# Scan stage of a Mamba layer: rows of C broadcast by DMA beside those of B, states written into PSUM

## The chip, the cores and the metric

One core of a Trainium2 chip runs the whole kernel in one launch. The metric is the time of one execution on the device in microseconds (us), measured several times, of which the median counts. The engines are TensorE (PE, its weight loads PEld), VectorE (DVE), ScalarE (ACT) and GpSimd (POOL); SyncE (SP) issues most DMAs.

## The reference, cut to what matters

The kernel computes a patch tokenizer (convolutions and depthwise convolutions on 32 images), a Mamba layer, and an attention layer with a mixture of experts. The change lies in the Mamba layer's selective scan, and touches the end of the tokenizer and the start of attention. There x is 32 sequences of 82 tokens and 192 channels, the inner width is 384, the state has 16 entries:

```python
xdbl = jnp.einsum('bld,kd->blk', z, W_xproj)
dt_in, Bm, Cm = jnp.split(xdbl, [DT_RANK, DT_RANK + D_STATE], axis=-1)
dt = jax.nn.softplus(jnp.einsum('blr,dr->bld', dt_in, W_dt) + b_dt)
A_bar = jnp.exp(dt[..., None] * A)
Bx = (dt * z)[..., None] * Bm[:, :, None, :]
# h[t] = A_bar[t] * h[t-1] + Bx[t], along the sequence
y = jnp.einsum('blds,bls->bld', h, Cm) + D_skip * z
```

## The kernel before

`mamba` works in 8 rounds of 4 sequences (N = 4 x 82 = 328 tokens). The 384 inner channels lie on 128 partitions three times over, so a full row of work is 3 x 328 = 984 elements. A round has 16 steps, one for each entry s of the state:

- ScalarE writes the decays exp(dt A_s) into PSUM banks 0 and 1 (`decays`, L1198), two steps ahead.
- GpSimd computes Bx, dt z times row s of B (`inputs`, L1450), up to three steps ahead in a ring of four tiles. It reads B from the tile `Bb`, in which row s stands on all 128 partitions.
- VectorE runs the scan in two halves of 492 elements (L1333), decays from PSUM and Bx from SBUF, into one of four SBUF tiles `hs`; then it multiplies that tile in place by row s of C (L1343), which it reads from PSUM.
- TensorE adds the product into banks 4 and 5 with an identity matrix (`add_y`, L1050) and, before that, spreads row s+2 of C over 128 partitions into bank 2 or 3, with a bf16 matmul of a one-hot matrix `sel` (`spread_c`, L1030). So that C keeps its precision it comes as three bf16 parts, stacked in the tile `P3` (the profile calls it P): the high part is copied by ScalarE (L1145), the rest R is computed by VectorE (L1289), its copies by ScalarE (L1149, L1150) and the last part by GpSimd (L1416).

Beside the scan of round i, the same 16 steps carry the parts of the round before and after it: `post` of round i-1 (drain of y by ScalarE at step 0, L1216; output projection at step 1, L997, and its addition on VectorE, L1309; norm; gated feed-forward at steps 10 to 13, L955, L1188, L1314, L1317; down projection at step 14, L1022, and additions, L1323) and `pre` of round i+1 (norm; gate and input projections at steps 3 to 5 with z on VectorE, L1285; the projection X at step 6, L979, from which B, C and the input of dt come; softplus in steps 8 to 11 with u by ScalarE, L1157, and four operations of GpSimd). For round 0, `pre` runs at the end of the tokenizer (the `tail` functions and the lines behind `tok.vector`), with softplus on VectorE (L1292 to L1302).

The order of the work on each engine is written out by hand. `program` (one for each engine) calls, for each step, `step`, `post` and `pre` in that order on VectorE and GpSimd, and `post`, `pre`, `step` on TensorE and ScalarE. Engines wait for one another by counting semaphores; a wait holds everything behind it on its engine. Side results use banks 6 and 7 in turn (`SIDE_TILES`, `free`). SP's own program (L887 and on) does, for each round: wait for the rows of B (`Bs`), store them to DRAM (L903), load them back in four groups of four rows, each broadcast to 128 partitions (L907), into one of two halves of `Bb`; then a fill of the experts' buckets with zeros (L917). Behind the last round stand the weight loads for attention (`fr.loads`).

After the last scan, GpSimd's `ending` fills tiles for attention with constants (`fills`, L681 to L685; L683 is the tile kB) and then computes roots for norms (L704).

`Own` and `at_least` are helpers for waits: `at_least` leaves out a wait for a value of zero or less.

## Time and profile before

| | us |
|---|---|
| median of 3 executions | 1364.94 (1364.93 to 1366.9) |
| the profiled execution, its own time | 1364.19 |
| its span, from the first to the last instruction | 1362.2 |
| TensorE busy | 1196.6 (88%) |
| VectorE busy | 1066.6 (78%) |
| ScalarE busy | 710.4 (52%) |
| GpSimd busy | 744.2 (55%) |

Busy times are of the whole span; stages have other shares. The eight rounds of the scan lie between about 253 and 763 us of the span, a round of the middle lasts 64.72 us. Times in the rows below count from the start of the span. In a timeline row stand start, duration, engine, line and operation, output and inputs with partitions x elements, how many instructions are merged (x), and in brackets for how long the engine stood idle before it and whose result ended that.

### The profile page before, as it was taken

The numbers are of one execution on the slowest core, as the hardware profiler recorded it, in microseconds if no ns is written. First come the engines' busy times: TensorE is split into PE (matmuls) and PEld (weight loads), VectorE is DVE, ScalarE is ACT, GpSimd is POOL, SyncE is SP. The second block draws the span as 40 slices with busy tenths as digits, with TensorE's granted clock in tenths as the row PEclk, the third lists the DMA queues.
The fourth block names the chain that finished last, engine by engine and source line by source line (L and its number), as shares of the span: only waits on it lengthen the run. The fifth ranks groups of instructions, "written<-read, shape, count | busy, mean of one in ns | idle before, by whom it ended". The sixth has DMA issues, their size and how long they took to land.

```text
span 1362.2 us, 20654 instructions
## 1 busy us (share of the span) xinstructions
PE 1196.6 (88%) x5844; PEld 759.2 (56%) x5845; DVE 1066.6 (78%) x2275; ACT 710.4 (52%) x1652; POOL 744.2 (55%) x473
## 2 busy tenths in 40 slices
PE   7986867478898989899997789999999889999996
PEld 4432434224454545455452468888888666667674
DVE  5998697998999999999989645677788756666663
ACT  1256431776868777787866334555553462323232
POOL 3047651877878796969697420115545665232322
PEclk9897878698999999999999998999998899999998
DMA  6200002440404041322320025001112133222221
GB/s 186 60 1 0 28 9 63 157 149 1 149 1 149 12 137 39 110 75 74 108 73 1 1 93 186 9 9 25 27 26 56 37 61 54 41 37 39 39 39 21
DMA packets 72573, 81.11 MB, mean 60 GB/s; under 512 B 13450, under 2 KB 65129, under 8 KB 72489
## 3 DMA queue, kind: packets, MB, share of 16 engines
q1 hardware_dynamic: 53154, 69.17, 16.0%
q0 software_dynamic: 17152, 9.24, 5.0%
q10 hardware_dynamic: 2184, 1.72, 0.5%
q8 instruction: 36, 0.59, 0.2%
q14 instruction: 47, 0.39, 0.1%
HBM read 48.75 MB, written 30.01 MB: 58 GB/s over the span
## 4 chain that ended last, share of the span: by engine, by line
PE 56%; DVE 20%; ACT 12%; issue 7%; POOL 2%; DMA 2%; DVEq 1%; SPq 0%; ACTq 0%; POOLq 0%
PE ps L1050 7%; PE ps L2295 6%; DVE hs L1333 5%; PE ps L2273 5%; PE ps L1652 3%; PE ps L1710 3%; PE ps L1022 3%; ACT ps L1198 3%; PE ps L2278 3%; PE ps L277 3%; PE ps L955 2%; PE ps L1725 2%; PE ps L2285 2%; PE ps L270 2%; PE ps L997 2%
## 5 line engine op out<-in xcount | busy, mean ns | idle before, releaser
L1450 POOL TENSOR_TENSOR Bx<-dtz,Bb 128x984 f32<-128x984 f32 x128 | 287.7, 2272 | 47.6 <-DVE hs L1333 34.4
L1333 DVE TENSOR_TENSOR_SCAN hs<-ps,Bx 128x492 f32<-128x492 f32 x256 | 287.7, 1165 | 15.9 <-POOL Bx L1450 12.2
L1050 PE MATMUL ps<-hs,b_id 128*128 128x492 f32 x512 | 236.9, 586 | 8.5 <-ACT y L1216 7.2
L1198 ACT ACTIVATE ps<-dt,A 128x324 f32<-128x324 f32 (+1 forms) x512 | 210.5, 456 | 56.3 <-DVE hs L1333 53.6
L2431 POOL DMA_INDIRECT out<-yt,dest x48 | 74.7, 1556 | 158.9 <-DVE yt L2417 149.2
L2350 ACT ACTIVATE hT__6147<-ps,e_b 128x128 f32<-128x128 f32 x288 | 79.4, 374 | 154.1 <-PE ps L2285 154.0
L1343 DVE TENSOR_TENSOR hs<-hs,ps 128x984 f32<-128x984 f32 x128 | 150.4, 1175 | 2.8 <-issue 0.6
L1050 PEld LDWEIGHTS ps<-hs,b_id 128*128 128x128 f32 x512 | 93.4, 195 | 75.3 <-issue 69.6
L2295 PE MATMUL ps<-W,hT__6147 128*128 x576 | 109.4, 327 | 1.0 <-DVE yb L2411 1.0
L2126 POOL DMA_INDIRECT buckets<-XS,c_slot x64 | 90.6, 1416 | 31.9 <-issue 16.4
L2138 POOL TENSOR_TENSOR c_x<-c_x,bro 82x192 f32<-82x192 f32 x32 | 18.9, 590 | 135.7 <-DVE c_x L1893 135.1
L2295 PEld LDWEIGHTS ps<-W,hT__6147 128*128 128x128 f32 x576 | 91.5, 191 | 1.7 <-issue 1.7
L1030 PE MATMUL ps<-P,sel 128*128 128x328 bf16 x128 | 40.2, 316 | 52.8 <-DVE hs L1343 40.8
L2397 DVE COPY hb<-ps 128x768 f32<-128x768 f32 x41 | 39.3, 958 | 59.2 <-PE ps L2278 58.1
L2273 PE MATMUL ps<-W,xT 128*128 x192 | 78.5, 534 | 6.1 <-DVE xT L2388 2.8
L1866 DVE TENSOR_REDUCE mx<-ps 82x12 f32<-82x984 f32 x32 | 37.7, 1178 | 56.0 <-PE ps L1710 55.3
L1030 PEld LDWEIGHTS ps<-P,sel 128*128 128x128 bf16 x128 | 12.3, 97 | 102.0 <-DVE hs L1343 67.4
L1725 PEld LDWEIGHTS ps<-V,PT 82*82 82x82 f32 x768 | 61.3, 154 | 7.6 <-issue 2.0
L1710 PE MATMUL ps<-kB,qT 128*82 128x328 f32 (+1 forms) x256 | 60.8, 382 | 3.1 <-DVE E L1870 2.0
L1725 PE MATMUL ps<-V,PT 82*82 82x17 f32 x768 | 60.3, 224 | 1.2 <-DVE XN L1900 1.2
L579 POOL TENSOR_TENSOR DF<-DF,prod 96x392 f32<-96x392 f32 x56 | 56.6, 1010 | 4.4
L207 DVE SCALAR_TENSOR_TENSOR ps<-PF,vec,ps 96x196 f32<-96x196 f32 (+2 forms) x168 | 57.7, 423 | 0.0
(291 smaller groups left out, 2520.6 us busy)
## 6 DMA issues: line engine op xcount, KB each, us to landing
Bb<-b_rows SPq DMA_DIRECT2D x32, 656.0 KB, 6.8
buckets<-b_zero SPq DMA_DIRECT2D x8, 2288.0 KB, 15.3
...
```

Of the source, the lines that this page charges most:

```text
L1050: mm = pe.matmul(ps[:, BANK_Y + h, 0:HALF], ident[:], f2(hs[:, s % LONG])[:, h * HALF:(h + 1) * HALF], start=s == 0, stop=s == STATE - 1)
L1198: a = act.activation(ps[:, BANK_A + h, c:c + w].rearrange("p (g t) -> p g t", t=S)[:, :, 1:S], dt[:, (par + t // STATE) % 2, m, g0 * S:g1 ...
L1333: v.tensor_tensor_scan(f2(hs[:, t % LONG])[:, c], ps[:, BANK_A + h, 0:HALF], f2(Bx[:, t % RING])[:, c], 0.0, ALU.mult, ALU.add).then_inc(s ...
L1343: v.tensor_tensor(hs[:, s % LONG], hs[:, s % LONG], ps[:, BANK_C + s % 2, 0:N].rearrange("p (a n) -> p a n", a=1).broadcast_to([128, NI, N ...
L1450: g.tensor_tensor(Bx[:, t % RING], dtz[:, p], Bb[:, p, t % STATE, :].rearrange("p (a n) -> p a n", a=1).broadcast_to([128, NI, N]), ALU.mu ...
L1710: mm = pe.matmul(ps[0:S, SCORES + h0 // 6, (h0 % 6) * S:(h0 % 6 + h1 - h0) * S], qT[:, par, m_, q * S:(q + 1) * S], kB[:, par, m_, q, j:j ...
L1725: mm = pe.matmul(ps[0:S, HEAD_OUT + c % 2, h * (DH + 1):(h + 1) * (DH + 1)], PT[:, c % 2, h, :], V[:, vpar, c, h, :], start=True, stop=True)
L2126: g.indirect_dma_start(out=xs, out_offset=bass.IndirectOffsetOnAxis(ap=slot[:, p % 2, k, c:c + 1], axis=0), in_=slots(p)[:, c, :], in_offs ...
L2273: pe.matmul(ps[:, UP + h, 0:384], xT[:, p, 0, :], W1[:, bass.ds(e, 1), h * 384:(h + 1) * 384].rearrange("p a n -> p (a n)"), start=True, s ...
L2295: mm = pe.matmul(ps[:, Y, 0:D], hT[:, p, k, :], W2[:, k, bass.ds(e, 1), :].rearrange("p a n -> p (a n)"), start=k == 0, stop=k == KF - 1)
L2350: a = act.activation(hT[:, p, k, :], ps[:, FLIPPED + k // 3, (k % 3) * 128:(k % 3 + 1) * 128], ACT.Gelu, bias=b1[:, k, bass.ds(e, 1)])
L2431: g.indirect_dma_start(out=out, out_offset=bass.IndirectOffsetOnAxis(ap=dest[:, p:p + 1], axis=0), in_=yt[:, p, :], in_offset=None, comput ...
```

## The change

- ScalarE copies the rows of B and C together out of PSUM into one tile `BCs` of 32 rows. SP stores them to DRAM and loads them back in four groups; a group brings four rows of B and four of C, on 128 partitions. The tile `BC` has room for one round (`Bb` had two halves with B alone), so from the second round on the load of a group waits for the product of the group's last state in the round before.
- `spread_c` goes, with its two calls ahead of the scan, the one-hot matrix (its load and its cast on VectorE), the tiles `P3`, `Pm`, `R` and what computes them.
- The scan writes its two halves into one place in PSUM, banks 2 and 3. So scan t waits until the product of state t-1 is done. The product reads the states from PSUM and C from `BC`, and writes to one of four SBUF tiles `hc`; it waits for the sum that used that tile four steps before.
- The bank of X is free when `dtin` is copied (before: when R was computed).
- `fills` waits for the last product before it clears kB, since kB takes the place of `BC`.
- The layout in SBUF follows; a spacer `room` keeps the tiles behind it where they were.

```diff
@@ attention_front @@
-    def fills(g):
+    def fills(g, rows_over):
         g.memset(nh[:], -0.5).then_inc(s_nh, 1)
         g.memset(V[:], 1.0).then_inc(s_cst, 1)
+        rows_over()
         g.memset(kB[:], 0.0).then_inc(s_cst, 1)
@@ mamba, tiles @@
-        oh = sb("oh", [128, 2 * STATE]); sel = sb("sel", [128, STATE, 128], BF16)
-        P3 = sb("P3", [128, 2, N], BF16); Pm = sb("Pm", [32, N], BF16); R = sb("R", [32, N]); Bs = sb("Bs", [STATE, N])
+        BCs = sb("BCs", [2 * STATE, N])
-        Bb = sb("Bb", [128, 2, STATE, N]); Bx = sb("Bx", [128, RING, NI, N])
-        hs = sb("hs", [128, LONG, NI, N]); skip = sb("skip", [128, NI, 128])
+        BC = sb("BC", [128, STATE // GROUP, 2, GROUP, N]); Bx = sb("Bx", [128, RING, NI, N])
+        hc = sb("hc", [128, LONG, NI, N]); skip = sb("skip", [128, NI, 128])
+        hs = ps[:, BANK_S:BANK_S + 2, :].rearrange("p a b -> p (a b)")[:, 0:NI * N]
-                      ("RG2", 1, s_z, 3, 3), ("RI2", 1, s_z, 3, 3), ("X", 1, s_R, 1, 1),
+                      ("RG2", 1, s_z, 3, 3), ("RI2", 1, s_z, 3, 3), ("X", 1, s_dtin, 1, 1),
@@ SP @@
-                sp.wait_ge(s_Bs, j + 1)
+                sp.wait_ge(s_BCs, j + 1)
                 if j >= 2:
                     sp.wait_ge(s_bx, (j - 1) * STATE)
-                sp.dma_start(b_d[par], Bs[:]).then_inc(s_bd, 16)
+                sp.dma_start(bc_d[par], BCs[:]).then_inc(s_bd, 16)
                 sp.wait_ge(s_bd, 16 * (j + 1))
+                rows = bc_d[par].rearrange("(a k g s) n -> a g k s n", a=1, k=2, s=GROUP)
                 for g in range(STATE // GROUP):
-                    rows = slice(g * GROUP, (g + 1) * GROUP)
-                    sp.dma_start(Bb[:, par, rows, :],
-                                 b_d[par, rows, :].rearrange("(a s) n -> a s n", a=1).broadcast_to([128, GROUP, N])).then_inc(s_Bb[g], 16)
+                    if j >= 1:
+                        sp.wait_ge(s_hc, (j - 1) * STATE + (g + 1) * GROUP)
+                    sp.dma_start(BC[:, g], rows[:, g].broadcast_to([128, 2, GROUP, N])).then_inc(s_BC[g], 16)
...
             sp.wait_ge(s_dt, ROUNDS)
-            sp.wait_ge(s_P3, ROUNDS)
             fr.loads(sp)
@@ TensorE @@
-            def spread_c(i, par, t):
-                at_least(pe, s_hc, i * STATE + t - 1)
-                if t % STATE == 0:
-                    pe.wait_ge(s_P3, i + t // STATE + 1)
-                pe.matmul(ps[:, BANK_C + t % 2, 0:N], sel[:, t % STATE, :], P3[:, (par + t // STATE) % 2, :],
-                          start=True, stop=True).then_inc(s_pc, 1)
...
             def step(i, par, s, last):
-                if not last or s + 2 < STATE:
-                    spread_c(i, par, s + 2)
                 add_y(i, par, s)
@@ ScalarE @@
-                    act.activation(Bs[:], ps[96:96 + STATE, bank("X"), 0:N], ACT.Copy).then_inc(s_Bs, 1)
-                    act.activation(P3[96:128, par, :], ps[96:128, bank("X"), 0:N], ACT.Copy).then_inc(s_hi, 1)
+                    act.activation(BCs[:], ps[96:96 + 2 * STATE, bank("X"), 0:N], ACT.Copy).then_inc(s_BCs, 1)
                     act.activation(dtin[:], ps[0:HD, bank("X"), 0:N], ACT.Copy).then_inc(s_dtin, 1)
-                if s == 7:
-                    act.wait_ge(s_R, j + 1)
-                    act.activation(P3[32:64, par, :], R[:], ACT.Copy)
-                    act.activation(Pm[:], R[:], ACT.Copy).then_inc(s_mid, 1)
@@ VectorE @@
-                if s == 6:
-                    v.wait_ge(s_hi, j + 1)
-                    v.tensor_tensor(R[:], ps[96:128, bank("X"), 0:N], P3[96:128, par, :], ALU.subtract).then_inc(s_R, 1)
...
                     if h == 0:
                         v.wait_ge(s_bx, i * STATE + (t + 1))
-                        at_least(v, s_ys, i * STATE + (t - LONG + 1))
+                        at_least(v, s_hc, i * STATE + t)
                     c = slice(h * HALF, (h + 1) * HALF)
-                    v.tensor_tensor_scan(f2(hs[:, t % LONG])[:, c], ps[:, BANK_A + h, 0:HALF], f2(Bx[:, t % RING])[:, c],
+                    v.tensor_tensor_scan(hs[:, c], ps[:, BANK_A + h, 0:HALF], f2(Bx[:, t % RING])[:, c],
                                          0.0, ALU.mult, ALU.add).then_inc(s_scan, 1)
...
                 v.wait_ge(s_scan, 2 * (i * STATE + s) + 2)
-                v.wait_ge(s_pc, i * STATE + (s + 1))
-                v.tensor_tensor(hs[:, s % LONG], hs[:, s % LONG],
-                                ps[:, BANK_C + s % 2, 0:N].rearrange("p (a n) -> p a n", a=1).broadcast_to([128, NI, N]),
+                at_least(v, s_ys, i * STATE + (s - LONG + 1))
+                v.tensor_tensor(hc[:, s % LONG], hs.rearrange("p (a n) -> p a n", a=NI),
+                                BC[:, s // GROUP, 1, s % GROUP, :].rearrange("p (a n) -> p a n", a=1).broadcast_to([128, NI, N]),
                                 ALU.mult).then_inc(s_hc, 1)
@@ VectorE, tail of the tokenizer @@
-                    v.tensor_copy(sel[:], oh[:, STATE:2 * STATE].rearrange("p (s a) -> p s a", a=1).broadcast_to([128, STATE, 128])).then_inc(s_cst, 1)
...
-                    v.memset(P3[64:96], 0.0)
                     v.memset(ps[:, BANK_A:BANK_A + 2, :], 0.0).then_inc(s_cst, 1)
...
             v.sem_inc(s_H, 2)
-            pre(0, 0, 6, None)
@@ GpSimd @@
-                if s == 7:
-                    g.wait_ge(s_mid, j + 1)
-                    g.tensor_tensor(P3[0:32, par, :], R[:], Pm[:], ALU.subtract).then_inc(s_P3, 1)
...
                 if t % GROUP == 0:
-                    g.wait_ge(s_Bb[t % STATE // GROUP], (i + t // STATE + 1) * 16)
+                    g.wait_ge(s_BC[t % STATE // GROUP], (i + t // STATE + 1) * 16)
...
                 g.wait_ge(s_bx, ROUNDS * STATE)
-                fr.fills(g)
+                fr.fills(g, lambda: g.wait_ge(s_hc, ROUNDS * STATE))
@@ places @@
-                       ("dtin", N * F), ("R", N * F), ("Bs", N * F), ("wzg", 4 * INNER * F), ("wx", NI * 128 * F + 544), ("wdt", INNER * F),
-                       ("sel", STATE * 128 * 2), ("Bb", 2 * STATE * N * F))
+                       ("dtin", N * F), ("BCs", N * F), ("room", N * F + 4096), ("wzg", 4 * INNER * F), ("wx", NI * 128 * F + 544), ("wdt", INNER * F),
+                       ("BC", 2 * STATE * N * F))
```

## Rows read from the trace of the kernel before

**Rows 1.** The page, part 4: the chain of waits by engine.

```profile
PE 56%; DVE 20%; ACT 12%; issue 7%; POOL 2%; DMA 2%; DVEq 1%; SPq 0%; ACTq 0%; POOLq 0%
```

**Rows 2.** Windows: length, busy by engine (instructions), PEclk, DMA share, GB/s.

```profile
383.70:448.50 64.80, 59.60 (x229) 32.34 (x228) 59.77 (x64) 48.35 (x115) 52.13 (x26) 1.00 0.25 79
...
718.00:721.40 3.40, 1.96 (x5) 0.73 (x5) 3.37 (x4) 2.43 (x8) 2.26 (x1) 1.00 0.00 0
```

**Rows 3.** Timeline of VectorE, a plain step.

```profile
293.79 1.18 DVE L1343 TENSOR_TENSOR hs<-hs,ps 128x984 f32<-128x984 f32 x1
...
294.88 2.25 DVE L1333 TENSOR_TENSOR_SCAN hs<-ps,Bx 128x492 f32<-128x492 f32 x2
...
297.17 1.18 DVE L1343 TENSOR_TENSOR hs<-hs,ps 128x984 f32<-128x984 f32 x1
```

**Rows 4.** Timeline of VectorE, stretch (i) of round 2.

```profile
408.83 0.50 DVE L1289 TENSOR_TENSOR R<-ps,P 32x328 f32<-32x328 f32 x1
...
414.20 2.25 DVE L1333 TENSOR_TENSOR_SCAN hs<-ps,Bx 128x492 f32<-128x492 f32 x2 [0.28 <-ACT ps L1198]
...
428.26 0.49 DVE L1314 SCALAR_TENSOR_TENSOR th<-th,ps 128x328 f32<-128x328 f32 x1 [0.84 <-ACT th L1188]
```

**Rows 5.** Timeline of TensorE and VectorE, stretch (ii).

```profile
380.08 0.30 PE L1030 MATMUL ps<-P,sel 128*128 128x328 bf16 x1
...
380.22 1.82 PE L1048 MATMUL ps<-z,skip 128*128 128x328 f32 x8
...
388.75 0.55 DVE L1309 TENSOR_TENSOR x<-xl,ps 82x384 f32<-82x384 f32 x1 [0.66 <-PE ps L997]
...
439.79 2.25 DVE L1333 TENSOR_TENSOR_SCAN hs<-ps,Bx 128x492 f32<-128x492 f32 x2 [1.07 <-POOL Bx L1450]
```

**Rows 6.** Timeline of VectorE, end of round 0.

```profile
309.59 2.26 DVE L1333 TENSOR_TENSOR_SCAN hs<-ps,Bx 128x492 f32<-128x492 f32 x2 [3.36 <-POOL Bx L1450]
```

**Rows 7.** Timeline of VectorE and ScalarE, before the first scan.

```profile
227.24 0.33 DVE L1365 MEMSET P<- 32x328 uint32 x1
...
233.70 0.50 DVE L1289 TENSOR_TENSOR R<-ps,P 32x328 f32<-32x328 f32 x1 [3.16 <-ACT P L1145]
...
239.88 1.02 ACT L1157 ACTIVATE u<-ax 128x984 f32<-128x984 f32 x1
...
244.42 0.73 DVE L1292 TENSOR_SCALAR ax<-u 128x984 f32<-128x984 f32 x1
...
253.01 2.25 DVE L1333 TENSOR_TENSOR_SCAN hs<-ps,Bx 128x492 f32<-128x492 f32 x2 [2.51 <-POOL Bx L1450]
```

**Rows 8.** Timeline of VectorE, two operations that wait for the one before.

```profile
245.19 1.18 DVE L1294 TENSOR_TENSOR ax<-u,ax 128x984 f32<-128x984 f32 x1
...
246.40 1.18 DVE L1296 TENSOR_TENSOR ax<-ax,rl 128x984 f32<-128x984 f32 x1
```

**Rows 9.** Groups by line, shapes apart: busy us, mean ns of one | idle us.

```profile
L207 DVE SCALAR_TENSOR_TENSOR ps<-PF,vec,ps 96x196 f32<-96x196 f32 x112 | 37.5, 415 | 0.0
...
L207 DVE SCALAR_TENSOR_TENSOR DF<-PF,vec,ps 96x196 f32<-96x196 f32 x16 | 5.9, 407 | 1.2 <-PE ps L277 1.2
```

**Rows 10.** DMA issues (part 6 of the page) and SP's timeline.

```profile
Bb<-b_rows SPq DMA_DIRECT2D x32, 656.0 KB, 6.8
...
235.61 1.91 SPq L907 DMA_DIRECT2D Bb<-b_rows  x4
```

**Rows 11.** Timeline of GpSimd, the end of the scan.

```profile
749.01 6.66 POOL L683 MEMSET kB<- 128x7872 f32 x1
...
775.62 2.91 POOL L704 TENSOR_TENSOR c_root<-c_root,c_nh 82x16 f32<-82x16 f32 x1 [18.45 <-DVE c_root L698]
```

**Rows 12.** Windows, the clock of TensorE in rounds 0 and after 7.

```profile
299.00:302.50 3.50, 1.37 (x4) 0.35 (x2) 3.29 (x3) 2.62 (x7) 3.50 (x2) 1.00 0.00 0
...
302.70:306.30 3.60, 2.47 (x6) 0.74 (x7) 3.43 (x3) 2.10 (x6) 3.52 (x2) 0.68 0.01 2
...
763.00:800.00 37.00, 31.39 (x136) 21.54 (x137) 17.84 (x81) 12.36 (x31) 12.65 (x5) 0.86 0.00 1
```

48 lines of the change are left out of this document (21 added, 27 removed).

## The prediction

> **What bounds the kernel now.** The page's chain of waits comes first [rows 1]: TensorE holds more than half of it over the whole kernel, but the change lies in the scan, and there another engine rules. In one whole round (first row of [rows 2]) TensorE is busy 59.60 and VectorE 59.77 of 64.80 us, ScalarE 48.35, GpSimd 52.13. The timeline tells which ends last where. A round has three stretches.
>
> (i) From its third product to its fifteenth VectorE runs back to back. A plain step starts a product at 293.79, the scans at 294.88 and the next product at 297.17 [rows 3]: 1.09 us from product to scan and 2.29 from scan to product, 3.38 in all. The other engines have their results in time, but for two short waits: 0.28 us for ScalarE's decays (414.20), and 0.84 us for a tanh that stands behind two table loads (428.26) [rows 4].
>
> (ii) From the last gated product of the feed-forward to the two additions of the projection, TensorE works almost without a gap: 28 to 32 down-projection passes, the sums over states 14 and 15 with the skip term, then, behind ScalarE's drain, the output projection. VectorE waits for it at 388.75 (0.66 us), and for GpSimd before that (1.07 us at 439.79) [rows 5].
>
> (iii) In the first round no feed-forward runs beside the scan. VectorE gets ahead and waits 3.36 us for GpSimd's Bx at 309.59 [rows 6]. Bx stands there behind the next round's softplus, all on GpSimd, which began when ScalarE's u came; this chain sets the end of round 0.
>
> Before all this, VectorE stands 3.16 us before the subtraction R (233.70), and everything up to softplus (244.42), the first Bx and the first scan (253.01) follows behind it in order [rows 7].
>
> **The change, part by part.**
>
> *The scan waits for the product.* All states now share one place, so scan t waits for product t-1 to finish. That wait never existed. A product lasts 1.18 us, but the scan starts 1.09 after it, overlapped [rows 3]. Where VectorE waits for its own result, the next one starts 0.03 us after the end: 245.19 + 1.18 = 246.37, next at 246.40 [rows 8]. So product to scan becomes 1.21: +0.12 us a step. The product's own wait for the scan is there already. Bounds: 0, and 0.15 if an unseen latency of PSUM doubles the gap. I take 0.12, as both engine and kind of instruction are the same. The Trainium skill (VectorE: DVE Perf Modes, section The DRAIN you can't avoid) says that a chain of Vector instructions takes as long with a semaphore after each as without, which would make this term nothing and the sum 10.6 us smaller. The trace disagrees, by the 0.12 us above, so the sum goes by the rows; the rule is rival B.
>
> *The scan writes to PSUM.* No scan here does. The nearest pair is the tokenizer's multiply-add, same shape and inputs, to PSUM 415 ns and to SBUF 407 [rows 9]: +8 ns, so +0.016 us for a step's two scans. From below -20 ns a scan (a write that drains sooner), from above +50 ns. The product only swaps which operand lies in PSUM; two of SBUF take 1.18 [rows 8], as does today's [rows 3]: nothing.
>
> Together a step grows by about 0.13 us wherever VectorE rules.
>
> *R, the bf16 thirds of C and their waits go.* VectorE loses R, 0.50 us a round (408.83) [rows 4]; ScalarE three copies; GpSimd one subtraction, for which it also stood waiting. ScalarE's relief takes away the 0.28 us wait, because its decays no longer stand behind those copies, and makes u earlier, so the 1.07 us wait for Bx [rows 5] goes too, but that lies in stretch (ii), where VectorE would then only wait longer for TensorE: nothing.
>
> *spread_c goes.* 128 small matmuls. In stretch (i) TensorE waits anyway: nothing. In stretch (ii) two of them stand in the row of work, each 0.14 us from its start to the next one's (380.08 to 380.22) [rows 5]: -0.28 us a round.
>
> *DMAs.* Each of 4 broadcasts a round doubles from 656 KB in 6.8 us [rows 10]. One buffer serves all rounds, so the load of group g waits for the product of its last state; on SP behind it stand the other groups and the zero fill of the buckets, needed long after. Group 0 of the next round is free at step 3, before its rows exist at step 6, and GpSimd needs it at step 13; group 3 comes free with the last product and is needed nine steps (30 us) later. If twice the bytes take 13.6 us, all are in time. Only at the start is it near: the loads go out from 235.61 [rows 10], and the first Bx, which now ends at 253.0 and lasts 2.3, will want group 0 at about 246.5, 11 us later. Between 6.8 and 13.6 us the cost is 0 to 2.6; I take 0, since the 6.8 us of today already hold the wait behind the three neighbours in the queue. SP's loads for attention now go out about a round's half later, some 90 us before their use: nothing.
>
> *Start.* VectorE no longer waits 3.16 us and computes no R (0.50) [rows 7]: the statistics move up 3.66. The memset of P's third (227.24) stood right before the z that the projection waited for; it and the gap behind it are 0.54. u, done at 240.90 (239.88 + 1.02), moves up by those 0.54 and by what ScalarE sheds, and VectorE is ready for it at 244.42 - 4.20 = 240.22: it is just there. The first Bx waits for dtz, the last link of VectorE's row, and the first scan for Bx (2.51) [rows 7]: both follow. Start: -4.2 us. The cast of sel, in the tokenizer, is hidden: behind it VectorE waits for the first z.
>
> *End.* GpSimd's memset of kB, 6.66 us at 749.01, now waits for the last product, about 763; with the next fill (1.5) it ends near 771.5. Its next work came at 775.62 after 18.45 us of idleness [rows 11]: covered, with 4 us to spare. Without that cover the roots of the layer norm would come late, one for one.
>
> *The sum*, against the profiled execution (span 1362.2, time 1364.19):
> - start -4.2
> - round 0: nine steps up to the u that starts GpSimd's chain, 9 x 0.13 = +1.2, R -0.5; the later steps fall into the 3.36 us wait; the two spreads -0.2
> - six rounds, 1 to 6: of 12 steps in stretch (i) one is swallowed by the tanh wait [rows 4], 11 x 0.13 = +1.43; less 0.50, 0.28 and 0.28: +0.37 each, +2.2
> - round 7: 13 steps, +1.7, nothing to take away
> - TensorE's clock: +0.7, half of the 1.4 us that one short fall near the end would cost (next part)
>
> Together +0.9: 1365.1 for that execution. The median of the three runs is 0.75 above it, so 1365.8.
>
> **The rivals.**
>
> *B. The new wait is free*, or hides behind the issue of the next instruction. 9 + 66 + 13 = 88 steps on the path, 88 x 0.12 = 10.6 us less: 1355.2. For it: wait and issue are cheap here (0.03 us [rows 8]). Against: the overlap of 0.09 us is in every step of the trace, and a wait must end it. 0.10.
>
> *C. The clock falls: slower.* In the quiet steps of round 7 TensorE is busy 1.96 of 3.4 us and keeps its full clock of 2.4 GHz (second row of [rows 2]); after 1.37 busy of 3.5 us in round 0 it fell, to an average of 0.68 in the next stretch, on its way to 1.2 GHz [rows 12]. Without spread_c and with the longer step it is busy 1.8 of 3.5: between the two. The Trainium skill (TensorE: Matmul & The Clock Gate, Part 1) says the throttled clock is the default and activity releases it, which speaks for this rival. In a quiet step a fall costs nothing: even at half speed the two matmuls of a state (1.96 less the spread's 0.14) fit in about 3.6. The place is the end of round 7: behind the last product TensorE's work lies bare, 31.39 us busy of 37.00 at 0.86 (last row of [rows 12]). A fall that takes another 3 to 10 us of it costs half of that (an estimate), 1.5 to 5 us, and as much again if stretch (ii) of a round is hit too: 1367.3 to 1374, say 1370. It decides from 2 us on. 0.17.
>
> *D. The scan is dearer in PSUM: slower.* 176 scans on the path; at +50 ns instead of +8 they cost 7.4 us more: 1373. It decides from 19 ns. For it: reading and writing PSUM at once, by an instruction with feedback, is in no row. Against: the multiply-add does read and write PSUM at once [rows 9]. 0.15.
>
> *E. The scan is cheaper there*, or the relief of ScalarE and GpSimd shortens stretch (i) by more than the one wait: at -20 ns a scan 176 x 0.028 = 4.9 us less, 1361. 0.12.
>
> *F. The larger broadcast is late* at the start: up to +2.6, 1368.4, for the most part still no change. 0.04.
>
> **How the numbers follow.** The forecast, no change that counts, has 0.42. A difference of 0.2% (2.7 us) is what a measurement of this kernel can tell from none. Faster: B 0.10, E 0.12, together 0.22. Slower: C 0.17, D 0.15 and 0.01 of F, together 0.33. Same: 0.45, the forecast with the other 0.03 of F. The predicted time is the forecast's, 1365.8. The range leaves out most of B and the far ends of C and D: 1357 to 1374; the forecast's own is 1362.5 to 1368.
>
> **What would show it.** Right: in the timeline of a plain step product to scan 1.21 and a step of 3.50 to 3.52; scans of 1.17 us; the first scan near 248.8; u, and with it the end of GpSimd's chain, only 3.5 us earlier than now; a round of 65.0 to 65.2 instead of 64.72; the last product at about the same time as today; the memset of kB behind it and over before the roots are wanted. Wrong: a plain step of 3.40 (B), scans of 1.20 (D), a granted clock below 1.00 in rounds 1 to 7 where it is 1.00 now (C), a wait of Bx for BC in any round (F), or a first scan that has not moved.

## The result, and the profile after

The changed kernel takes 1389.87 us (median; 1382.89 to 1394.33), the one before, on the same chip in turn with it, 1365.92: a ratio of 1.0161, with an interval of 1.0107 to 1.0216. A second series of both gave 1391.23 against 1368.09, 1.0165 (1.013 to 1.020). The forecast was 1365.8 with 1357 to 1374 around it; the time lies 16 us above that range. Times are medians; the ratios, here and below, leave out one execution, of e1, that took 1475 us at a granted clock of 0.81. Each ratio is against the kernel before run in the same series, and its median moved between series (1361.6 to 1368.1), so kernels of different series are compared by their ratios.

The chain of waits and the costliest groups, from the page of the kernel after (busy us, mean ns of one | idle us before them and what ended most of it), beside [rows 1]:

```profile
PE 53%; DVE 25%; issue 11%; ACT 7%; POOL 2%; DMA 1%; DVEq 1%; SPq 0%; ACTq 0%; POOLq 0%
...
L1312 DVE TENSOR_TENSOR_SCAN ps<-ps,Bx 128x492 f32<-128x492 f32 x256 | 289.7, 1177 | 24.9 <-ACT ps L1180 6.0
...
L1322 DVE TENSOR_TENSOR hc<-ps,BC 128x984 f32<-128x984 f32 x128 | 150.6, 1176 | 13.4 <-issue 10.7
...
BC<-bc_rows SPq DMA_DIRECT2D x32, 1312.0 KB, 6.8
```

"Issue" has grown from 7 to 11% of the chain, and the product, which before hardly ever waited, has 10.7 us of it in front of it. The scan lasts 1177 ns (1165 before). A broadcast twice as large lands in the same 6.8 us.

A plain step, from VectorE's timeline, beside [rows 3]; then the first scan and the end of round 0, beside [rows 6, 7]:

```profile
285.02 1.18 DVE L1322 TENSOR_TENSOR hc<-ps,BC 128x984 f32<-128x984 f32 x1
286.34 2.26 DVE L1312 TENSOR_TENSOR_SCAN ps<-ps,Bx 128x492 f32<-128x492 f32 x2
288.63 1.18 DVE L1322 TENSOR_TENSOR hc<-ps,BC 128x984 f32<-128x984 f32 x1
...
245.82 2.26 DVE L1312 TENSOR_TENSOR_SCAN ps<-ps,Bx 128x492 f32<-128x492 f32 x2 [2.52 <-POOL Bx L1423]
...
303.95 2.26 DVE L1312 TENSOR_TENSOR_SCAN ps<-ps,Bx 128x492 f32<-128x492 f32 x2 [2.84 <-POOL Bx L1423]
```

Product to scan is 1.32 us here (1.30 to 1.32 in round 0, 1.28 in the rounds of the loop), not 1.09 and not the forecast's 1.21; the step is 3.61 us. The first scan comes 7.2 us sooner in this pair of profiles; 2.4 us of that lie ahead of any work that the change touches (see the part on the prediction).

So far nothing makes 24 us. The clearest marks in the trace are the eight starts of ScalarE's drain of y (L1216 before, L1198 after), one at the end of each round (us, read from ScalarE's timeline of each kernel):

| round | 0 | 1 | 2 | 3 | 4 | 5 | 6 | 7 |
|---|---|---|---|---|---|---|---|---|
| before | 319.01 | 383.73 | 448.45 | 513.18 | 577.89 | 642.61 | 707.32 | 766.69 |
| after | 312.79 | 378.53 | 452.50 | 520.63 | 594.63 | 663.36 | 729.11 | 791.51 |

Rounds 1 and 6 take 65.74 and 65.75 us after the change, against 64.72. But rounds 2 and 4 take 73.97 and 74.00, rounds 3 and 5 68.13 and 68.73. On VectorE, ScalarE, TensorE and GpSimd the rounds 1 to 6 are a loop of three passes of two rounds, so the ends of rounds 2 and 4 are where that loop branches back; SyncE's instructions run straight on. The timeline of all engines there, after (weight loads left out):

```profile
438.75 0.36 SPq L909 DMA_DIRECT2D BC<-bc_rows  x1
438.82 2.26 DVE L1312 TENSOR_TENSOR_SCAN ps<-ps,Bx 128x492 f32<-128x492 f32 x2
...
439.15 0.47 SPq L918 DMA_DIRECT2D buckets<-b_zero  x1
...
446.76 1.18 DVE L1322 TENSOR_TENSOR hc<-ps,BC 128x984 f32<-128x984 f32 x1 [5.23 <-issue]
...
452.50 0.99 ACT L1198 ACTIVATE y<-ps 128x984 f32<-128x984 f32 x1 [10.53 <-issue]
...
453.63 2.80 PE L1041 MATMUL ps<-hc,b_id 128*128 128x492 f32 x3 [9.40 <-ACT y L1198]
454.42 2.26 DVE L1312 TENSOR_TENSOR_SCAN ps<-ps,Bx 128x492 f32<-128x492 f32 x2 [2.81 <-ACT ps L1180]
```

and before:

```profile
409.79 1.92 SPq L907 DMA_DIRECT2D Bb<-b_rows  x4
411.76 0.47 SPq L917 DMA_DIRECT2D buckets<-b_zero  x1
...
446.58 1.18 DVE L1343 TENSOR_TENSOR hs<-hs,ps 128x984 f32<-128x984 f32 x1 [0.40 <-issue]
...
448.45 0.99 ACT L1216 ACTIVATE y<-ps 128x984 f32<-128x984 f32 x1 [1.83 <-PE ps L1050]
```

After the change VectorE stands 5.23 us, and ScalarE 10.53 us, before an operation whose inputs have long been there; no other engine ends that time ("issue"). In the same 15 us run the load of group 3 and the zero fill, which SP now issues at the last product of the round, 438.75 and 439.15, and which used to be under way from 409.79. Windows of the stretch after (length, busy by engine, PEclk, DMA share, GB/s):

```profile
446.00:454.00 8.00, 0.36 (x1) 0.40 (x2) 4.63 (x4) 1.50 (x3) 2.26 (x1) 0.64 0.82 247
454.00:458.00 4.00, 4.00 (x7) 1.83 (x7) 2.26 (x2) 4.00 (x11) 1.24 (x1) 0.50 0.00 0
747.00:750.60 3.60, 1.92 (x4) 0.68 (x4) 3.43 (x4) 3.11 (x9) 3.60 (x2) 1.00 0.00 0
```

TensorE idles nearly through the first 8 us and is at 1.2 GHz (0.50) when it has to catch up. That is the tail of the stall, in rounds 3 and 5: their third product starts 9.82 and 10.42 us after the drain, that of the other rounds 7.43, and from then on all rounds are alike. The third row is a quiet step of round 7: 1.92 us busy of 3.60 and the full clock.

The balance against the profile before: first scan -7.2; round 0 +1.0; six rounds of +1.03, +6.2; the four disturbed ones another 284.83 - 4 x 65.74 = +21.9; round 7 (62.40 against 59.37) +3.0; together +24.8 at the last drain, and 5.3 in the stages behind, to a span of 1392.3. In a second profile of the same kernel (a1, below) the disturbed rounds cost 20.4 us.

### The profile page after: what moved, and what is told of

It reads as the page before. It is cut to its first block, busy times and chain, and to the rows that moved or that the text cites. A ratio compares the mean times of both kernels' runs of the same rounds, so it can differ in the third digit from the quotient of the medians.

```text
span 1392.3 us, 20343 instructions
## 1 busy us (share of the span) xinstructions
PE 1200.0 (86%) x5716; PEld 757.3 (54%) x5717; DVE 1071.3 (77%) x2265; ACT 706.1 (51%) x1628; POOL 738.1 (53%) x465
## 4 chain that ended last, share of the span: by engine, by line
PE 53%; DVE 25%; issue 11%; ACT 7%; POOL 2%; DMA 1%; DVEq 1%; SPq 0%; ACTq 0%; POOLq 0%
DVE ps L1312 6%; PE ps L2268 6%; DVE hc L1322 6%; PE ps L2246 5%; PE ps L1041 5%; PE ps L1625 3%; PE ps L1022 3%; PE ps L2251 3%; PE ps L1683 3%; PE ps L2258 3%; PE ps L1698 2%; PE ps L277 2%; PE ps L955 2%; PE ps L997 2%; PE ps L270 2%
## 5 line engine op out<-in xcount | busy, mean ns | idle before, releaser
L1423 POOL TENSOR_TENSOR Bx<-dtz,BC 128x984 f32<-128x984 f32 x128 | 288.3, 2270 | 110.7 <-DVE ps L1312 78.8
L1041 PE MATMUL ps<-hc,b_id 128*128 128x492 f32 x512 | 249.5, 611 | 77.1 <-DVE hc L1322 52.3
L1312 DVE TENSOR_TENSOR_SCAN ps<-ps,Bx 128x492 f32<-128x492 f32 x256 | 289.7, 1177 | 24.9 <-ACT ps L1180 6.0
L1180 ACT ACTIVATE ps<-dt,A 128x324 f32<-128x324 f32 (+1 forms) x512 | 215.0, 457 | 63.1 <-DVE ps L1312 58.0
L1041 PEld LDWEIGHTS ps<-hc,b_id 128*128 128x128 f32 x512 | 91.2, 194 | 189.6 <-issue 121.9
L1322 DVE TENSOR_TENSOR hc<-ps,BC 128x984 f32<-128x984 f32 x128 | 150.6, 1176 | 13.4 <-issue 10.7
L955 PE MATMUL ps<-hfT,wug 128*128 128x328 f32 x128 | 44.6, 472 | 20.4 <-DVE av L1296 19.0
L207 DVE SCALAR_TENSOR_TENSOR ps<-P,vec,ps 128x196 f32<-128x196 f32 x168 | 56.4, 420 | 0.0
```

The lines of the kernel that those rows point to most:

```text
L207: i = eng.scalar_tensor_tensor(flat(dst[:, k, cols]) if t == 8 else acc, tap(src, k, c, t, a, b), w, acc, ALU.mult, ALU.add)
L1041: mm = pe.matmul(ps[:, BANK_Y + h, 0:HALF], ident[:], f2(hc[:, s % LONG])[:, h * HALF:(h + 1) * HALF], start=s == 0, stop=s == STATE - 1)
L1180: a = act.activation(ps[:, BANK_A + h, c:c + w].rearrange("p (g t) -> p g t", t=S)[:, :, 1:S], dt[:, (par + t // STATE) % 2, m, g0 * S:g1 ...
L1312: v.tensor_tensor_scan(hs[:, c], ps[:, BANK_A + h, 0:HALF], f2(Bx[:, t % RING])[:, c], 0.0, ALU.mult, ALU.add).then_inc(s_scan, 1)
L1322: v.tensor_tensor(hc[:, s % LONG], hs.rearrange("p (a n) -> p a n", a=NI), BC[:, s // GROUP, 1, s % GROUP, :].rearrange("p (a n) -> p a n" ...
L1423: g.tensor_tensor(Bx[:, t % RING], dtz[:, p], BC[:, t % STATE // GROUP, 0, t % GROUP, :].rearrange("p (a n) -> p a n", a=1).broadcast_to([ ...
```

## The experiments

Three theories stood at the start. **T1**: each engine has to fetch its code anew where the loop branches back, and the moved load and fill delay these fetches. **T2**: the longer step is the whole loss. **T3**: twice the broadcast bytes slow everything, wherever they run. Beside them the question of what the new wait costs, and why.

**The moved DMAs, one and both out of the way.** e1 issues the fill behind group 0's load, e2 gives the last load three more products:

```diff
@@ SP, e1_fill_early @@
                     sp.dma_start(BC[:, g], rows[:, g].broadcast_to([128, 2, GROUP, N])).then_inc(s_BC[g], 16)
+                    if j >= 1 and g == 0:
+                        sp.dma_start(xs[j * part:(j + 1) * part, :]...).then_inc(s_zf, 16)
@@ SP, e2_both_later @@
-                        sp.wait_ge(s_hc, (j - 1) * STATE + (g + 1) * GROUP)
+                        sp.wait_ge(s_hc, (j - 1) * STATE + (g + 1) * GROUP + (3 if g == 3 else 0))
```

> The changed kernel, but from round 1 on SyncE issues the 2.3 MB zero fill of the buckets right behind the load of group 0 (mid-round, as before the change) and no longer behind the load of group 3; that last load (1.3 MB) still starts at the last product of the round. T1 (the stalls at the back branch of the loop, at the ends of rounds 2 and 4, are instruction fetches that stand behind the moved DMAs): more than half of the bytes in the way are gone, so the drains of y of rounds 2 and 4 come 2 to 6 us earlier each against the one before than in the changed kernel (74.0 us for round 2 there), and the total falls by 8 to 20 us, to 1370 to 1382. T2 (the whole loss is the longer step: 104 to 128 steps by 0.23 us): nothing changes, 1387 to 1392. T3 (twice the broadcast bytes slow everything, wherever they run): nothing changes, or worse.

> The changed kernel, but the load of group 3 waits for three more products (those of the next round), so that it and the zero fill behind it start some 11 us past the round's end and past the loop's branch. T1: the stalls at the ends of rounds 2 and 4 go, and with them the cold clock of TensorE in the rounds behind them; the loss against the kernel before is left with 0.1 to 0.25 us a step and the gain at the start: 1365 to 1373. T2: 1387 to 1392, no change. T3: no change, and the fill, later by 11 us, may meet the pool's reads: 1387 to 1395.

Measured: e1 1379.28, ratio 1.0093 (1.0057 to 1.0129); e2 1372.18, 1.0056 (1.0030 to 1.0082). T2 and T3 fall, as the totals dropped. The drain of round 2 in the timeline of e1, then VectorE's product and the drain in that of e2:

```profile
448.12 0.99 ACT L1203 ACTIVATE y<-ps 128x984 f32<-128x984 f32 x1 [5.80 <-issue]
```

```profile
442.52 1.18 DVE L1322 TENSOR_TENSOR hc<-ps,BC 128x984 f32<-128x984 f32 x1 [1.20 <-issue]
...
445.64 0.99 ACT L1198 ACTIVATE y<-ps 128x984 f32<-128x984 f32 x1 [3.87 <-issue]
```

The less DMA at the branch, the shorter the stall: 10.53, 5.80, 3.87 us. But 3.87 are left with no data moving at all, where T1 had the stall go, and the kernel before had none. T1 is not the whole.

**The fill at the branch of the kernel before.**

```diff
@@ SP, the kernel before @@
+                if j >= 1:
+                    sp.wait_ge(s_hc, j * STATE)
                 part = BUCKET_ROWS // ROUNDS
                 sp.dma_start(xs[j * part:(j + 1) * part, :]...).then_inc(s_zf, 16)
```

> The kernel before, with the zero fill of rounds 1 to 7 held until the last product of the round before, so that 2.3 MB start at each round's end; the broadcasts of B stay where they were. T1: the stall at the back branch appears in the kernel before too: idle time with no releaser of 3 to 10 us on VectorE and ScalarE at the ends of rounds 2 and 4, and the total grows by 8 to 20 us, to 1373 to 1385. T2 and T3 (no bytes and no step are added): 1363 to 1368.

A miss for T1 as it stood: 1364.55, ratio 0.9999 (0.9968 to 1.0030), every round 64.72. The fill goes out at the branch, and VectorE's product waits as good as nothing:

```profile
445.82 0.39 SPq L919 DMA_DIRECT2D buckets<-b_zero  x1
...
449.00 1.18 DVE L1345 TENSOR_TENSOR hs<-hs,ps 128x984 f32<-128x984 f32 x1 [0.60 <-issue]
```

So 2.3 MB on their way to DRAM at the branch do not make this kernel slower. That they delay no fetch is not shown. The trace lists pieces of 8 KB of kind "instruction" on DMA queue q14. In e4 the piece ahead of VectorE's product starts at 446.68 us and the fill's first packet at 446.79, so that piece was already under way. The next one comes 4.55 us after VectorE ran out of work, against 0.77 us in the kernel before; nothing waited for it. Something else makes the changed kernel open to such delays.

**The branch taken away.** In e7 (the changed kernel) and e8 (the one before):

```diff
@@ program @@
-            with engine.Fori(0, (ROUNDS - 2) // 2) as t:
+            for t in range((ROUNDS - 2) // 2):
```

> The changed kernel with the loop over rounds 1 to 6 written out (same instructions, same waits, same DMAs, no branch at the ends of rounds 2 and 4). T1, as it stands after the first four runs (the branch stalls VectorE and ScalarE, by 1.2 and 3.9 us even where no DMA is under way, and by 5 and 10 us where the moved load and fill are): all rounds take the 65.75 us of the undisturbed ones, none has idle time without a releaser over 1 us, the 8.2 + 2.4 us of rounds 2 and 3 and the same of 4 and 5 go, 21 us in all: 1366 to 1372. T4 (the moved DMAs delay every instruction fetch at the round's end, the branch has no part): the code runs straight, but fetches stand behind the same bytes, so a stall of 3 to 10 us appears at the ends of some rounds, perhaps more of them: 1380 to 1400.

> The kernel before with the same loop written out, as a control. Its rounds were all 64.72 us, the one stall at the branch 0.4 us: no change, 1360 to 1366, if T1 holds; a gain of more than 3 us would say that the branch cost the kernel before something that I have not seen.

e7: 1369.91, 1.0048 (1.0021 to 1.0076), all six rounds 66.06 to 66.07 us, although both DMAs still start at the end of each. The whole stall needs the branch, and goes with it; T4, that the moved DMAs delay every fetch at a round's end, falls. (The rounds are 0.3 us longer than the undisturbed 65.75; product to scan is 1.31 us in the code written out and 1.28 in the loop, and eleven steps of 0.03 make that.) e8: 1365.15, 1.0026 (1.0003 to 1.0048), rounds 64.48: the branch had cost the kernel before next to nothing, as expected; that its total did not follow is taken up below.

**Where the loop's code lies.** A row of waits that are long fulfilled, on each engine ahead of the loop, moves the loop's code and nothing else:

```diff
@@ program; e9: e2 with 32, e9b: e2 with 64, e13: the kernel before with 64, e15: the changed kernel with 32 @@
             late()
+            for _ in range(32):
+                engine.wait_ge(s_cst, 2)
```

> The kernel of the run e2_both_later with 32 waits that are long fulfilled put ahead of the loop on each engine: the loop's code lies 32 instructions further on, nothing else changes. T5 (what the branch costs depends on where its source and target lie in the pieces in which the instructions are fetched: 8 KB each in the trace, three of them around the branch in the kernel before and six in the changed one): ScalarE's idle time of 3.87 us without a releaser at the ends of rounds 2 and 4 changes by over 1 us in either direction. If the branch costs the same wherever it lies, it stays within 0.3 us of 3.87 on ScalarE and of 1.2 on VectorE.

> The same with 64 waits. T5: another value again, and it may be zero; if the branch costs the same wherever it lies, 3.87 and 1.2 us as before.

> The kernel before with 64 fulfilled waits ahead of the loop on each engine. T5: its branch, free but for 0.4 us on VectorE, may now cost 1 to 5 us at the ends of rounds 2 and 4, seen as idle time without a releaser, and those rounds take 65 to 68 us in place of 64.72. If the branch is dear only in the changed kernel, for a reason in its waits, the rounds stay at 64.72 and the total at 1360 to 1368.

> The changed kernel with the 32 fulfilled waits ahead of the loop and nothing else: the load of group 3 and the zero fill still start at the end of each round. If the place of the code decides alone, both stalls go: rounds 65.75, total 1367 to 1372. If only the number of fetches is the code's place and their length the DMAs' doing, ScalarE's idle time falls from 10.5 to at most 5 us, VectorE's stays near 5 (5.23 in the changed kernel, 1.07 with the DMAs moved away), the rounds 2 and 4 take 68.5 to 71 us and the total is 1373 to 1381.

Measured: e9 1369.49 (1.0051, 1.0029 to 1.0072), e9b 1372.13 (1.0058, 1.0030 to 1.0087), both with six rounds of 65.74 or 65.75; e13 1362.83 (1.0000, 0.9973 to 1.0028), rounds 64.72; e15 1377.62 (1.0075, 1.0045 to 1.0106), its disturbed rounds 69.99 and 70.05 (3 and 5 here: the stalled product stands behind the drain). The drain of round 2 in e9, then the drain and the product behind it in e15:

```profile
445.25 0.99 ACT L1200 ACTIVATE y<-ps 128x984 f32<-128x984 f32 x1 [2.30 <-PE ps L1043]
```

```profile
443.37 0.99 ACT L1200 ACTIVATE y<-ps 128x984 f32<-128x984 f32 x1 [2.30 <-PE ps L1043]
...
445.80 1.18 DVE L1324 TENSOR_TENSOR hc<-ps,BC 128x984 f32<-128x984 f32 x1 [5.18 <-issue]
```

With 32 or 64 instructions in front, ScalarE's stall is gone altogether, even (e15) with the load and the fill under way; it waits for TensorE as it does in every round. VectorE's is not: 1.07 and 1.21 us in e9 and e9b, which lie hidden, and 5.18 in e15. The DMA views of the 11 to 18 us around the first branch, the line of the instruction queue q14 (packets, MB, share): after (e2 has six as well), then e9 (e15 has two as well), then e6, which is the changed kernel with one wait of VectorE moved (below).

```profile
q14 instruction: 6, 0.05, 0.8%
```

```profile
q14 instruction: 2, 0.02, 0.5%
```

```profile
q14 instruction: 3, 0.02, 0.4%
```

The count of pieces does not measure the stall. The kernel before has three and one of another queue, and ScalarE does not stall; e6 and e5 (below) have three too, with both DMAs at the branch, and ScalarE stands 10.27 and 10.53 us, while VectorE, whose product waits 5.23 us in the changed kernel, goes straight on:

```profile
446.13 1.18 DVE L1323 TENSOR_TENSOR hc<-ps,BC 128x984 f32<-128x984 f32 x1
453.15 0.99 ACT L1198 ACTIVATE y<-ps 128x984 f32<-128x984 f32 x1 [10.27 <-issue]
```

The times of the pieces say more. Where VectorE's product waits with "issue" at the branch, a piece ends 1.6 to 1.8 us before it starts, in every kernel with the loop: 444.96 and 446.76 after the change, 440.88 and 442.52 in e2, 444.97 and 446.58 before. Without the load that piece starts 0.7 to 1.8 us before VectorE has run out of work; with the load in flight 2.3 to 3.4 us after (after, a1, e1, e15). It lasts 0.3 to 0.7 us in all of them. So the fetch comes late; the piece itself is not slow. (The trace does not say whose code a piece holds; the times do.)

So there are two causes. The place of the code sets which engine stands before a fetch; the DMAs in flight set how late that fetch comes. ScalarE's stall needs its unlucky place, and grows with the traffic, from 3.87 to 10.53. VectorE's is 0.2 to 1.3 us without the load, hidden, and 4.4 to 5.5 with it (e1, the load alone, 4.64), except in e5 and e6, where it has none. Each branch costs, over the two rounds around it, 10.9 us with both causes (10.2 in a1), 4.3 with the DMAs alone (e15), 3.2 with the place alone (e2), nothing with neither (e9): the two together cost more than their sum. In whole times the place alone doesn't show: e2 has 1.0056, e9 1.0051 and e9b 1.0058.

That a taken branch stalls for its code is what the Trainium skill says (Runtime: NRT & Kernel Launch, section Instruction fetch mechanics): prefetch is sequential, and a branch to code that is not in the engine's window has to fetch it before execution goes on. The traces agree, with 3.87 us for ScalarE at one place of the code and nothing 32 instructions further on; that such a fetch stands behind other DMA traffic they add themselves. Of e13 I had expected more than it showed: 64 instructions moved the code of the kernel before as well and cost nothing, so I can't say which places are unlucky.

**What the new wait costs.** e3 is the kernel before with the wait alone; e6 the changed kernel with that wait first; e16 is e6 with the loop written out.

```diff
@@ scan; e3, in the kernel before @@
                         at_least(v, s_ys, i * STATE + (t - LONG + 1))
+                        at_least(v, s_hc, i * STATE + t)
@@ scan; e6, in the changed kernel @@
                 for h in range(2):
+                    if h == 0:
+                        at_least(v, s_hc, i * STATE + t)
                     v.wait_ge(s_ab, 2 * (i * STATE + t) + (h + 1))
                     if h == 0:
                         v.wait_ge(s_bx, i * STATE + (t + 1))
-                        at_least(v, s_hc, i * STATE + t)
```

> The kernel before, with one wait added and nothing else: the scan also waits for the semaphore of VectorE's own last product, as in the changed kernel. If the wait itself costs what the changed kernel shows (the gap between product and scan 0.14 us against 0.03), the plain step grows from 3.38 to about 3.5 us (its end is set by the product, the scan pair and that gap) and the total by 128 x 0.12, some 10 to 15 us, less what TensorE's stretches hide: 1373 to 1380. If the gap is due to the scan that reads or writes PSUM otherwise, the gap stays at 0.03 and the total at 1363 to 1368.

> The changed kernel with the scan's wait for VectorE's own product put ahead of its waits for the decays and for Bx. If the gap of 0.14 us between product and scan is a queue of waits that are looked at one after the other once the product is done, only the self-wait's place changes: gap 0.08 to 0.12 and the total 2 to 6 us lower. If the gap is the time from the product's last write to the scan's start whenever the scan must not overlap it, it stays 0.14 and the total at 1385 to 1392.

> The changed kernel with the self-wait first among the scan's waits, as in e6, and the loop written out, as in e7. In e6 product to scan was 1.21 us in rounds 0 and 7, whose waits have constant values, and 1.40 in the rounds of the loop, whose values are in registers; with the self-wait last it is 1.31 and 1.28. If it is the registers' arithmetic that stands behind the wait in the loop, product to scan is 1.21 in every round here, the plain step 3.51, the rounds 64.4 to 65.0 (66.07 in e7), and the total 1361 to 1367. If the loop's rounds pay for another reason (their feed-forward), they keep 1.40, rounds of 67, total 1375 to 1380.

e3: 1377.56, ratio 1.0110 (1.0076 to 1.0144). Its plain step, then the same of e6 in round 0, of e6 inside the loop, and of e16 inside what was the loop:

```profile
289.12 1.18 DVE L1344 TENSOR_TENSOR hs<-hs,ps 128x984 f32<-128x984 f32 x1
290.43 2.25 DVE L1334 TENSOR_TENSOR_SCAN hs<-ps,Bx 128x492 f32<-128x492 f32 x2
292.72 1.18 DVE L1344 TENSOR_TENSOR hs<-hs,ps 128x984 f32<-128x984 f32 x1
```

```profile
285.78 1.18 DVE L1323 TENSOR_TENSOR hc<-ps,BC 128x984 f32<-128x984 f32 x1
287.00 2.26 DVE L1313 TENSOR_TENSOR_SCAN ps<-ps,Bx 128x492 f32<-128x492 f32 x2
...
353.22 1.18 DVE L1323 TENSOR_TENSOR hc<-ps,BC 128x984 f32<-128x984 f32 x1
354.62 2.26 DVE L1313 TENSOR_TENSOR_SCAN ps<-ps,Bx 128x492 f32<-128x492 f32 x2 [0.22 <-DVE hc L1323]
```

```profile
352.72 1.17 DVE L1323 TENSOR_TENSOR hc<-ps,BC 128x984 f32<-128x984 f32 x1
353.93 2.26 DVE L1313 TENSOR_TENSOR_SCAN ps<-ps,Bx 128x492 f32<-128x492 f32 x2
```

The wait costs 0.21 to 0.22 us a step in a kernel whose scan writes to SBUF (e3: 1.31 from product to scan, 3.60 a step), so it is the wait and not PSUM. Its place counts: as the last it makes 1.31 us, the last of four in e3 and of three in the changed kernel, whose rounds in the loop have 1.28. As the first of three it makes 1.21 where the awaited values are constants, and 1.40 inside the loop, where they are computed in registers. Written out (e16), it is 1.21 in every round, 3.51 a step, 64.98 a round. These are the forecast's own numbers (1.21, 3.50 to 3.52, 65.0 to 65.2). Why the last place costs 0.10 more with constant values isn't shown; the number of waits, three or four, made no difference. e6 itself took 1397.31 (1.0256, 1.0209 to 1.0302), outside both readings of its expectation: in the loop the wait's early place made the step longer. e16 took 1370.62 (1.0056, 1.0031 to 1.0080); its rounds came out as expected, its total did not.

**C by DMA alone.** The states go back to SBUF:

```diff
@@ scan and step, in the changed kernel @@
-                        at_least(v, s_hc, i * STATE + t)
+                        at_least(v, s_ys, i * STATE + (t - LONG + 1))
-                    v.tensor_tensor_scan(hs[:, c], ps[...], ...
+                    v.tensor_tensor_scan(f2(hc[:, t % LONG])[:, c], ps[...], ...
-                at_least(v, s_ys, i * STATE + (s - LONG + 1))
-                v.tensor_tensor(hc[:, s % LONG], hs.rearrange("p (a n) -> p a n", a=NI),
+                v.tensor_tensor(hc[:, s % LONG], hc[:, s % LONG],
```

> The changed kernel, but the scan writes its states into the SBUF ring again, the product works in place there with C from the DMA'd rows, and the scan waits for TensorE's additions instead of VectorE's own product. If VectorE's operation with both inputs in SBUF and GpSimd's work do not get into each other's way, the plain step goes back to 3.35 to 3.4 us (scan 1.165, product 1.17, gap 0.03) and the total falls by up to 128 x 0.23 less TensorE's stretches, to 1370 to 1378 with the branch stalls still in it. If they share a port and shut each other out, the product lasts up to as long as GpSimd's own operation (2.27 us) besides its 1.18, or GpSimd's grows: the step is 3.8 to 5 us and the total 1400 to 1500.

1461.35, ratio 1.0721 (1.0675 to 1.0766), rounds of 73 to 75 us where nothing stalls. The two groups of its page that changed:

```profile
L1422 POOL TENSOR_TENSOR Bx<-dtz,BC 128x984 f32<-128x984 f32 x128 | 349.3, 2743 | 102.5 <-DVE hc L1312 76.4
...
L1321 DVE TENSOR_TENSOR hc<-hc,BC 128x984 f32<-128x984 f32 x128 | 256.8, 2006 | 2.1
```

The same product that takes 1176 ns with one input in PSUM takes 2006 on average with both in SBUF, and Bx 2743 instead of 2270. It is the company that does it: the 21 products beside which GpSimd does nothing take 1.18 us, the 92 that overlap a Bx take 2.25 on average. The Trainium skill has this (SBUF — State Buffer, section Who interferes with whom): a tensor_tensor with both inputs in SBUF contends with a GpSimd instruction that reads SBUF. The trace agrees that each lengthens the other. The states in PSUM are thus what keeps C by DMA from costing 7%, and the wait is their price: with no room for a second set of states in the eight banks, scan and product take turns.

**All together.** e12 writes the loop out and cuts the product in two parts that count separately, so the first half's scan waits only for the first part; e14 keeps the loop, with that product, 32 fulfilled waits and the later load.

```diff
@@ scan @@
-                        at_least(v, s_hc, i * STATE + t)
+                    at_least(v, s_hc, 2 * (i * STATE + t) + (h - 1))
@@ step @@
-                v.tensor_tensor(hc[:, s % LONG], hs...[all], BC...[128, NI, N], ALU.mult).then_inc(s_hc, 1)
+                for a, b in ((0, NI - 1), (NI - 1, NI)):
+                    v.tensor_tensor(hc[:, s % LONG, a:b], hs...[:, a:b], BC...[128, b - a, N], ALU.mult).then_inc(s_hc, 1)
```

> The changed kernel with the loop written out and the product with C in two parts, 656 and 328 columns; each counts by itself, so the scan of the first half waits for the first part while the second is still running, and TensorE adds the first half one part earlier. If the self-wait costs what the runs so far show (product to scan 1.31 us against 1.09 without it, the same in the kernel before with only that wait added), the second part hides it: product to scan is 0.75 + 0.41 = 1.16 us by the rate of one column a 0.96 GHz cycle, the plain step 3.45 (3.61 now), the rounds 64.0 to 65.0 (66.07 now) and the total 1355 to 1363, at or below the kernel before. If each part brings its own gap of 0.14, the step is 3.65 to 3.75 and the total 1370 to 1378.

> All that the runs so far point to, in one kernel: the changed kernel with its loop kept, 32 fulfilled waits ahead of it (ScalarE's branch then cost nothing), the load of group 3 three products later (none of it at the branch), and the product in two parts (plain step 3.45 us in e12). Rounds of 64.0 to 64.3 us, no idle time without a releaser over 1.5 us at the ends of rounds 2 and 4, last drain of y near 760. If what follows the scan takes the 594 to 598 us of most profiles, the total is 1355 to 1359 and the kernel beats the one before by 0.3 to 0.5%. If it takes the 602 to 603 of e8 and e12 (TensorE's clock at half level for longer there), 1364 to 1367: no gain, and then an earlier end of the scan is taken back by the stage behind it.

> The changed kernel itself, once more, beside these: 1385 to 1394 us, stalls at the ends of rounds 2 and 4 as in its first profile (VectorE 5.2, ScalarE 10.5), rounds 74.0 there; what follows the last drain of y tells whether its 600.8 us of the first profile or the 594 to 598 of most others is usual.

The parts do what they should; e12's timeline:

```profile
282.53 1.25 DVE L1325 TENSOR_TENSOR hc<-ps,BC 128x656 f32<-128x656 f32 x2
283.69 2.25 DVE L1314 TENSOR_TENSOR_SCAN ps<-ps,Bx 128x492 f32<-128x492 f32 x2
285.98 1.25 DVE L1325 TENSOR_TENSOR hc<-ps,BC 128x656 f32<-128x656 f32 x2
```

1.16 us from product to scan and 3.45 a step, as worked out; rounds of 64.29 us in both, the last drain at 759.56 and 761.22, against 766.69 in the kernel before. But the totals are 1366.48 (1.0031, 1.0012 to 1.0051) and 1365.97 (0.9984, 0.9966 to 1.0003): e14 is the best form of the change, and can't be told from the kernel before. e12's expectation had 1355 to 1363, a miss; of e14's two cases the second came true, 1364 to 1367 and no gain. a1 repeated the changed kernel: 1391.23, the stalls at 5.18 and 10.48 us, and 596.6 us from the last drain to the end of the span, against 600.8 in its first profile.

**Where that gain goes.** The 7.1 and 5.5 us by which these drains come sooner are not all gain. VectorE's last pair of additions in the tokenizer (L491) lies ahead of all that the change touches there but a hidden cast, and starts anywhere between 217.3 and 225.2 us in the 18 profiles. Counted from it, the last drain comes at (us; the stage is that from the last drain to the first down projection of an expert):

| | before | e4 | e13 | e8 | e16 | e12 | e14 | e9 | after |
|---|---|---|---|---|---|---|---|---|---|
| drain | 543.6 | 543.7 | 543.7 | 542.2 | 543.2 | 539.8 | 539.7 | 549.0 | 570.8 |
| stage | 324.0 | 331.0 | 331.1 | 330.2 | 330.7 | 330.7 | 330.8 | 325.4 | 328.7 |

So e12 and e14 gain 3.9 us in the scan, 0.3%, and e16 0.4. In the stage TensorE is busy 95% and its work is the same in all kernels; windows before, e12, e13:

```profile
766.69:1090.60 323.91, 307.37 (x2347) 250.58 (x2346) 228.84 (x719) 156.25 (x294) 121.53 (x105) 0.94 0.17 49
```

```profile
759.56:1090.10 330.54, 311.77 (x2347) 253.10 (x2346) 229.94 (x719) 156.27 (x294) 124.36 (x108) 0.93 0.17 48
```

```profile
767.45:1098.50 331.05, 315.56 (x2348) 256.41 (x2347) 228.63 (x719) 156.16 (x294) 121.71 (x105) 0.92 0.17 48
```

The stage lasts 320 to 331 us and tends to be longer where the granted clock is lower; length times clock is 302 to 308 us, so the clock is only part of it. An earlier end of the scan is not needed for a long stage: e4 and e13, whose scans are those of the kernel before and end at 769 and 767 us, have the longest. So whether an execution has 324 or 331 us there moves its total by 0.5%, whatever the scan did. e14's 0.9984 fits its gain of 0.3%; e12 at 1.0031 and e16 at 1.0056 are 8 us longer than their scans say, e8 at 1.0026 is 5 us longer, and why stays open.

## Why the prediction was wrong

**The DMA paragraph is the step that failed.** It priced the moved load of group 3 and the zero fill behind it at nothing, since their data are needed long after. That is true of the data: no Bx waits for BC in any round. What it did not ask is what else uses the DMA queues at the new time. The two now start at the loop's back branch, where the engines fetch code, and together with the loop's new place in the code they cost 21.9 us in this profile. In whole times e7, without the branch, has a ratio of 1.0048 and e9, with both causes moved, 1.0051, against 1.0161: 1.1% or 15 us. Either would be 1372 to 1373 beside this kernel before, within the range. The forecast listed no branch among its rivals, and its sum had no term for one. All of the miss above the range is this.

**The term of the new wait was mis-sized.** The mechanism was right (a wait ends the overlap of product and scan, and rival B, a free wait, is wrong), the size 0.12 was taken from two operations with a single wait each [rows 8]. As the last of the scan's waits it costs 0.19 us in the loop of the changed kernel and 0.21 to 0.23 elsewhere. e3 against the kernel before: 64.72 to 66.74 a round, +2.0 where the forecast had +1.4; 62.22 against 59.37 in round 7, +2.9 where it had 1.7. What the Trainium skill says of a chain of tensor_copy, that a semaphore after each costs nothing extra (VectorE: DVE Perf Modes, section The DRAIN you can't avoid), does not carry over to this product and scan, by those 0.21 us.

**The scan in PSUM**: +12 ns (1177 against 1165) where +8 was forecast; e3, with the wait but states in SBUF, has 1168. Rival D is wrong, and so is E's cheaper scan; of E's relief there is a little at the start (below).

**R, the thirds of C and spread_c**: forecast -0.50, -0.28 and -0.28, -1.06 a round; the changed kernel's undisturbed round is 65.75 and that of e3 66.74: -0.99. Right. Together with the wait, a round was to grow by 0.37 and grew by 1.03.

**Start**: forecast -4.2, and a first scan near 248.8; it came at 245.82. From VectorE's last pair of additions in the tokenizer to the first scan it is 29.92 to 30.00 us in the five profiles with the old front and 25.15 to 25.17 in the thirteen with the new one: -4.8. The rest of the 7.2, 2.4 us, lies ahead of that point (223.07 against 220.67), which scatters from 218.0 to 225.2 us in the old kernels and from 217.3 to 223.7 in the new. The forecast's two terms are right, 3.8 us for the wait and R (3.66) and 0.5 for the memset (0.54). What it left out is 0.5 us in the product dtz, whose inputs both lie in SBUF: it ran beside the subtraction of the last third of C on GpSimd, and that is gone. Before, with GpSimd's row, then after:

```profile
247.84 1.62 POOL L1416 TENSOR_TENSOR P<-R,Pm 32x328 bf16<-32x328 f32 x1
248.84 1.67 DVE L1302 TENSOR_TENSOR dtz<-dt,z 128x984 f32<-128x984 f32 x1
...
242.12 1.18 DVE L1281 TENSOR_TENSOR dtz<-dt,z 128x984 f32<-128x984 f32 x1
```

It is 1.67 us in all five old fronts and 1.18 in all thirteen new ones: the same collision that e5 has in every round.

**Round 0**: +0.5 forecast, +1.0 measured, GpSimd's chain still at its end (2.84 us at 303.95).

**End**: the memset of kB runs behind the last product and is over before the roots are wanted. Right:

```profile
787.89 6.66 POOL L684 MEMSET kB<- 128x7872 f32 x1 [14.94 <-DVE hc L1322]
794.50 1.48 POOL L685 MEMSET XS<- 82x1664 f32 x1
```

**The clock (rival C)** stayed at 1.00 in the quiet steps, with 1.92 us busy of 3.60; it fell, to 0.50, only behind the stalls (10.2 us each) and, as before, in round 0. A clock below 1.00 in the rounds 1 to 7 was the forecast's sign of C; here it follows from the stalls and is not the cause. The forecast's +0.7 for the clock is half of 1.4 us that none of its rows gives. The broadcast (rival F) was in time.

With these sizes the forecast's own sum, stalls aside, would have been -4.8 + 1.0 + 6 x 1.03 + 3.0 = +5.4 us, 1370.3; e9, the changed kernel with the load later and its code moved, without the stalls, measured +0.51%, 7 us. Slower would have been the right side even without the branch, though within the range.
